# A state-space scan interleaved with expert bodies on one core: the next batch's scan preparation is placed earlier, and the scan tiles are dealt out differently

## What is computed

```python
x = x + tanh(g_xattn[0]) * ssm(ctx_1024, layernorm(x))
x = x + tanh(g_ffn[0]) * moe(layernorm(x))

# ssm: in_proj, causal conv of 4 taps, u = silu(.), x_proj -> dt_lo, Bm, Cm
delta = softplus(einsum('er,brl->bel', dt_proj_w, dt_lo) + dt_proj_b)
def step(state, xs):                      # 512 channels x 16 states, over 512 steps
    dA = exp(d_t[..., None] * A)
    state = state * dA + (d_t * u_t)[..., None] * B_t[:, None, :]
    y_t = einsum('ben,bn->be', state, C_t)
y = (y + D * u) * silu(z)
# moe: softmax router, top 6 of 64, 8 experts with low-rank adapters, and a shared expert
```

## Time and profile before

| | us |
|---|---|
| median of 3 runs | 1624.6 |
| lowest and highest | 1622.92, 1626.42 |
| the profiled execution | 1626.78 |
| its span | 1624.7 |
| busy: PE, DVE, POOL, ACT | 1514.8, 1164.5, 733.2, 658.2 |
| the scan of the first batch, before the first body | about 190 |
| ten bodies of the first batch | 412 |
| of the second, third, fourth | 347, 346, 327 |

### The profile page before, as it was taken

How to read it: one execution, slowest core, us unless ns; L and a number is a source line. 1 busy time by engine, 2 the same in 40 slices (tenths; PEclk the granted TensorE clock), 3 DMA queues, 4 the chain that set the end, 5 groups by cost and what they waited for, 6 DMA issues and landing times.

```text
span 1624.7 us, 19150 instructions
## 1 busy us (share of the span) xinstructions
PE 1514.8 (93%) x6440; PEld 1146.8 (71%) x6440; DVE 1164.5 (72%) x1635; ACT 658.2 (41%) x1035; POOL 733.2 (45%) x536
## 2 busy tenths in 40 slices
PE   5678699988888999999999999999999999999999
...
GB/s 262 264 331 316 190 148 240 194 315 302 286 290 278 260 260 154 248 276 292 239 243 286 226 168 174 253 315 272 279 253 240 176 194 247 226 207 251 255 240 99
DMA packets 144945, 395.99 MB, mean 244 GB/s; under 512 B 25456, under 2 KB 66672, under 8 KB 129616
## 3 DMA queue, kind: packets, MB, share of 16 engines
...
## 4 chain that ended last, share of the span: by engine, by line
PE 58%; DVE 19%; issue 7%; ACT 7%; POOL 5%; DMA 2%; ACTq 1%; SPq 0%; DVEq 0%; POOLq 0%
PE b_g L815 14%; PE b_u L815 13%; PE b_u L909 7%; DVE ring L1615 6%; PE b_q L909 3%; PE b_g L909 3%; DVE ring L1621 3%; PE b_q L863 3%; PE b_g L881 3%; DVE tt L1589 2%; POOL ring L1514 2%; PE b_u L848 2%; PE b_g L848 2%; POOL yx L1523 2%; POOL gm L1459 1%
## 5 line engine op out<-in xcount | busy, mean ns | idle before, releaser
L1514 POOL TENSOR_TENSOR ring<-du,rep 128x512 f32<-128x512 f32 x256 | 346.0, 1359 | 111.5 <-DVE du L1694 81.5
L815 PE MATMUL b_g<-xnb,gm 128*128 128x512 f32 (+1 forms) x1440 | 353.8, 395 | 1.1 <-DVE xnb L1592 1.1
L815 PE MATMUL b_u<-xnb,gm 128*128 128x512 f32 (+1 forms) x1440 | 350.0, 392 | 1.0 <-DVE xx L1589 0.9
L1615 DVE TENSOR_TENSOR_SCAN ring<-b_a,ring 128x512 f32<-128x512 f32 x256 | 310.7, 1214 | 15.0 <-ACT b_a L1056 14.4
L1523 POOL TENSOR_TENSOR yx<-yx,ring 128x512 f32<-128x512 f32 x192 | 260.9, 1359 | 121.8 <-DVE ring L1621 121.3
L815 PEld LDWEIGHTS b_g<-xnb,gm 128*128 128x128 f32 (+1 forms) x1440 | 256.6, 180 | 78.9 <-issue 8.6
L815 PEld LDWEIGHTS b_u<-xnb,gm 128*128 128x128 f32 (+1 forms) x1440 | 256.8, 179 | 74.3 <-DVE xx L1589 3.0
L1056 ACT ACTIVATE b_a<-delta,cs 128x512 f32<-128x512 f32 x256 | 173.5, 681 | 112.1 <-DVE ring L1615 111.9
L1589 DVE SCALAR_TENSOR_TENSOR tt<-tt,b_g 128x512 f32<-128x512 f32 (+1 forms) x120 | 81.9, 683 | 169.3 <-ACT tt L1056 168.7
L909 PE MATMUL b_u<-dwt,hhl 128*128 128x512 f32 (+1 forms) x720 | 191.7, 395 | 0.9 <-issue 0.5
L1056 ACT ACTIVATE tt<-b_g 128x512 f32<-128x512 f32 (+1 forms) x120 | 71.1, 593 | 248.1 <-PE b_u L848 206.1
...
## 6 DMA issues: line engine op xcount, KB each, us to landing
...
rep<-bc_d ACTq DMA_DIRECT2D x64, 512.0 KB, 7.1
...
qat<-scr_qa SPq DMA_DIRECT2D x25, 512.0 KB, 9.3
...
```

Source lines behind the costliest of these rows:

```text
L815: i = mm(out_b[0:IW[m], :], w, v, start=(n == 0), stop=(n == 11 and not is_routed(s)))
L1514: v.tensor_tensor(ring_at(nb, T), du[:, T % 4, :], rep[:, N % NREP, 0], ALU.mult).then_inc(pool_dbu, 1)
L1615: v.tensor_tensor_scan(w, ba[T % 2][:], w, 0.0, ALU.mult, ALU.add).then_inc(dve_scan, 1)
```

## The change

The same operations, with the same sizes, in another order; `delta_u` becomes two operations of 128x1024 in place of one of 128x2048.

- PE: `in_proj(2, 3)` stands before the third chunk's gate product instead of behind it. `x_proj` stands before `up(s, 0, 1)` of `shared_1` instead of before `up(s, 2, 1)`; `dt_proj` stands around `up(s, 1, 1)`, instead of behind `qa` and behind the third `down`.
- ACT and DVE: the preparation's steps follow to match. `exp_abs`, `rep_load`, `one_plus`, `rest_of_w`, `log_w` and the subtraction behind it (`log_part`) move from e0 and the end of `shared_1` into `shared_1`, ahead of `aw_first`; `softplus`, `delta_u`, `d_u` and the first `exp_tile` stand at the head of e0.
- Tiles: e0 9, e1 10, e2 to e6 9 each, one in each slot (e0 has two in c and none in a; e1 has two in a).
- POOL: in e0 the splits of the next body's weights stand between the tiles, as in the other bodies.

```diff
         def first_tile(e):
-            return 0 if e == 0 else 4 + 10 * (e - 1)
+            return (0, 9, 19, 28, 37, 46, 55)[e]
+        SLOTS = ("a", "h0", "b", "h1", "c", "h2", "d", "e", "f")
+        FIRST_BODY = {"h0": 1, "b": 1, "h1": 1, "c": 2, "h2": 1, "d": 1, "e": 1, "f": 1}
...
@@ PE, shared_0 @@
                 up(s, 1, 1).then_inc(pe_gu, 1)
+                if pre_:
+                    in_proj(b + 1, (2, 3))
                 up_waits(s, 2)
                 up(s, 2, 0)
                 up(s, 2, 1).then_inc(pe_gu, 1)
-                if pre_:
-                    in_proj(b + 1, (2, 3))
...
@@ ACT, shared_1 @@
+                exp_flat(b)
+                if pre_:
+                    state_rows(b + 1)
+                tanh(s, 0)
+                h_hi(s, 0)
+                soft_rows(b)
+                if pre_:
+                    dt_evac(b + 1, (0, 1))
+                tanh(s, 1)
+                if pre_:
+                    dt_evac(b + 1, (2, 3))
+                h_hi(s, 1)
+                if pre_:
+                    exp_abs(b + 1)
+                    for n in range(NREP):
+                        rep_load(b + 1, n)
                 tanh(s, 2)
                 h_hi(s, 2)
+                if pre_:
+                    log_w(b + 1)
                 aw_hi(s + 1)
...
@@ POOL, e0 @@
-                    at = (2, 4, 6, 8) if e > 0 else (0, 0, 1, 2)
+                    at = (2, 4, 6, 8) if e > 0 else (1, 3, 5, 7)
...
@@ DVE, shared_0 @@
                 route(b)
+                if pre_:
+                    conv(b + 1, 0)
                 hidden(s, 1)
                 if pre_:
-                    conv(b + 1, 0)
+                    conv(b + 1, 1, (0, 1))
                 hidden(s, 2)
                 if pre_:
-                    conv(b + 1, 1)
-                    make_u(b + 1, (0, 1))
+                    conv(b + 1, 1, (2,))
+                    make_u(b + 1, range(HC))
```

113 lines of the change are left out of this document (46 added, 67 removed).

## The result

The changed kernel takes 1618.8 us (median of 5, 1615.96 to 1618.94), the kernel before beside it 1626.08; the ratio is 0.9947 (0.9933 to 0.9961). It is faster by 0.5%, and 20 us slower than forecast, outside the range. Its profiled execution took 1615.96 us, span 1614.1, the shortest of the five, so lengths read from it flatter the change a little.

A forecast was written before the change was run, and what follows sets the result against it. Fourth-batch bodies are PE-bound at 33.5 us; DVE bounds the first batch's routed bodies, with waits in e0, e3, e4. Batches -12.6, -7.5, -6.4 sum to -26.5: 1600.3 from the profiled run, 1598.1 by the median; forecast 1599, range 1589 to 1613.

The forecast's parts named there:

- Tiles out of e2 to e6: First batch: five bodies lose one tile, 1.7 us each; with shifted waits, e1 to e6 -10.5 us, bounds 0 and -17.
- ACT's rounding of dw: First batch, slot a: with one tile there, rounding and tanh wait for no scan, some 1.3 us each in e2, e5.
- (1): Rival: transfers hold the first batch, so half its remaining gain is left; 1605 us, chance 15%.
- (2): Rival: waits in the shared bodies go to PE at once in three batches; at 2 us each 1605, chance 10%.
- (5): Rival: no change, because DVE's total work is the same; chance 3%.
- The bound of -17: First batch, e1 to e6: the gain if these bodies came down to PE's 36 us.
- e0, first batch: Preparation's DVE operations leave or move behind add_down, five tiles come in: 43.7 to 41.3 us, -2.4, bounds -4.0 and +1.5.
- e0, second and third: The qat wait and late add_down go: 39.7 to 37.0 us, -2.7 each, bounds -2.8 and +1.
- e3: Second and third batch: loses 1.7 us of DVE, gains a copy's wait of about 1 us; 34.7, -1.0.
- e4: Second and third batch: loses the tile and both copies' waits, reaching 33.5 us; -4.1 and -3.0.
- Shared bodies: No idle PE before, so only loss possible: hidden 2's low part later in shared_0, +0.3 us three times, +0.9.
- u's chain: shared_1: make_u, u_hi, u_lo start earlier and should end at 638.3, 1.5 us before x_proj wants them.

The follow-up runs named there:

- run 9: Changed kernel with GpSimd's own pieces in e2 to e6 of the first batch one tile earlier in its order: 1609.5 us, ratio 0.9890.
- run 3: Changed kernel with the raw weights of the first batch's routed experts loaded to a quarter only (wrong results): whole kernel 1615.5 us.
- run 7: Changed kernel with the tiles dealt as in the kernel before and the preparation in its new place: 1622.2 us, ratio 0.9980.
- run 12: Changed kernel with w_d and ws_d stores ahead of gm1's load and rep's loads back at the end of shared_1: 1610.9 us, ratio 0.9893.
- run 2: Changed kernel with c_copy behind the tanh instead of directly ahead of it in slots a, b and c: 1617.5 us, ratio 0.9941.
- run 13: Changed kernel with GpSimd's pieces of e2 to e6 one tile earlier, stores ahead of gm1's load and rep's loads back: 1602.9 us, ratio 0.9852.
- run 14: Changed kernel with GpSimd's pieces earlier, stores ahead of gm1's load, rep's loads back, and c_copy behind the tanh: 1598.7 us, ratio 0.9827.

## Why the prediction was wrong, point by point

- **Tiles out of e2 to e6 (-10.5 for e1 to e6; measured -0.2): the step that failed.** The term 5 x 1.7 took one tile out of VectorE's order and left everything beside it in place. VectorE's busy time fell from 229.9 to 220.7 us, as computed. But GpSimd's pieces, counted from the body's first tile, stayed while VectorE's steps came a tile earlier, and both engines' two-input operations then waited for each other: hidden 2's low part took 2.30 us instead of 1.05 in e4, dwt's 2.65 instead of 1.75. With the pieces shifted (run 9) the six are 8.5 us shorter, and the five tiles are worth 8.1 to 9.0 against the old deal. The other fault of the term is its place: it counted a tile as worth the same wherever it stood, and slot a, where VectorE waits for TensorE's product and tanh 0 anyway, gave 3.8 of the 8.5 us (4.5 with the pieces shifted). So the size of the term was right for a kernel in which GpSimd's pieces move too, and wrong for this one. The prediction used that rule of the Trainium skill ("SBUF — State Buffer", section "SBUF: two separate sides") where it favoured the change, in e0, and not here, where it spoke against it. By that rule the trace agrees: the fences of run 9 show both engines waiting the other out.
- **ACT's rounding of dw (1.3 us each in e2 and e5).** It did leave the tanh's way, but VectorE's idle time ahead of hidden 0 was 0.36 us in e2 before and is 1.84 after, 1.52 and 1.21 in e5: there was little to take away in e2, and TensorE's product holds the tanh next.
- **The rivals.** None had it. (1) names transfers, which are worth 1.9 us at most in run 3; nearest in time are (1) with (2), 1611, and (5), 1626, and neither mechanism was found. The bound of -17 rested on 36 us of TensorE's need; with the pairs below it is that of the later batches, 33.5.
- **e0, first batch (-2.4; measured -5.2).** Right in direction and in mechanism: run 7, with the preparation moved and the old deal, has 37.9. The size is outside its bound of -4.0, because TensorE's need was put too high, at 39.7 us: twelve of the matmuls counted are the other halves of pairs that run at once (below), and without them the same sum gives 36.9. The two delta<-delta,z take 2.35 us together in their new place, 1.2 each, against 4.56 in the earlier trace rows.
- **e0, second and third (-2.7 each; with e1 measured +0.4 and -0.9, and worse in the other traces).** The second step that failed. The wait for qat went, as said. The failed step is the queue: x_proj and dt_proj ahead of `up(s, 1, 1)` delay gm1's load (16.3 us into shared_1 instead of 11.5), and it and rep's loads fall on the stores of w_d and ws_d, behind whose landing SP waits. The wait moved from qat to awt. TensorE's need of 36.9 us was the right floor (37.17 in run 12), but 0.8 us of the forecast gain were only the mark between e0 and e1. A small slip beside it: 3 x 512 KB at 262 GB/s are 6 us, not 5.
- **e3 (-1.0; measured +0.4).** The copy's wait ahead of hidden 0 was counted. The one in slot c was taken to cost what the one in h1 had cost before; it stands ahead of tanh 2, and run 2, which moves both copies, gives 1.0 back. **e4 (-4.1, -3.0; measured -4.0, -2.9):** right, with its two rows. **Shared bodies (+0.9; measured +1.2), u's chain, dt_proj:** right. TensorE waits for none of them in shared_1, and 0.4 us for hidden 2's low part in shared_0.
- **Fourth batch (0; measured -2.8).** Not seen: its `soft_lo` moved up as well, so the last store leaves 15.0 us into shared_1 instead of 17.8. But it landed after 4.6 us instead of 2.4, and the loads behind began only 0.6 us earlier, so how the rest comes about is open. A part of it is scatter: with the same code this body took 37.0 to 38.6 us in the runs up to 11, by the wait for awt (0.6 to 1.8 us).

With both clashes taken out the kernel stands at 1602.9 us (run 13), and at 1598.7 with the copies moved too (run 14), against 1599 forecast. That this is the forecast's number is in part luck. By the table, run 14 has 3.9 us more than forecast in e0 of the first batch and 3.8 in the fourth, where nothing was forecast; it has 5.0 less in the other rows (1.4 in e1 to e6 of the first batch, 2.0 in e0 with e1, 0.8 in e3, 0.5 in e4, 0.3 in the shared bodies). It also holds three edits that the forecast kernel does not have.
